# Turning W inside the sort and ordering layer 1 part by part in a two-layer conditional kernel

## The reference

```python
# x: 128 x 64 x 512; itok_B_0_7 ("subject") and itok_B_0_6 ("adapter"): one index in 0..7 and 0..6 per batch item
out0 = einsum('bct,bcd->bdt', x, w[subject]) + bias[subject][:, :, None]        # w: 8 x 64 x 64
x = x + out0
H = einsum('btd,od->bto', x, W)                                                # W: 512 x 512
xa = einsum('btd,brd->btr', x, A[adapter])                                     # A: 8 x 16 x 512
x = x + H + einsum('btr,bor->bto', xa, Bm[adapter]) * scalings[adapter]        # Bm: 8 x 512 x 16
```

## Time and profile before

| | us |
|---|---|
| median of 3 runs (246.84 to 247.28) | 247.12 |
| the profiled execution | 246.9 |
| its span, first to last instruction | 245.2 |
| TensorE busy in the span | 231.0 |
| VectorE, ScalarE, GpSimd busy | 148.5, 109.9, 71.7 |

### The profile page before, as it was taken

One profiled execution on the slowest core, in us unless ns is written; L12 is line 12 of the kernel. 1 busy time (PEld: TensorE's weight loads), 2 busy tenths in 40 slices (PEclk: granted clock), 3 DMA queues, 4 the chain that ended last, 5 costly groups with the idle time before them and its releaser, 6 DMA issues.

```text
span 245.2 us, 9843 instructions
## 1 busy us (share of the span) xinstructions
PE 231.0 (94%) x2917; PEld 188.8 (77%) x2919; DVE 148.5 (61%) x258; ACT 109.9 (45%) x191; POOL 71.7 (29%) x280
## 2 busy tenths in 40 slices
PE   1889999999999999999999999999999999999990
PEld 1667888888887888888888888888888888887750
DVE  6778856774457736775457736675457735345642
ACT  3265462552535353552535353562536343444621
POOL 3456501560046301560045501564134330000000
PEclk9999999999999999999999999999999999999998
DMA  6846564745465574745456563746455463641323
GB/s 143 264 137 144 172 179 130 208 118 166 135 178 141 153 192 110 215 121 178 125 164 152 150 196 107 210 114 192 127 153 161 136 195 111 199 124 45 88 54 77
DMA packets 23621, 36.56 MB, mean 149 GB/s; under 512 B 6066, under 2 KB 6066, under 8 KB 23602
## 3 DMA queue, kind: packets, MB, share of 16 engines
q1 hardware_dynamic: 16544, 26.36, 39.2%
q10 hardware_dynamic: 7058, 9.97, 14.1%
HBM read 19.53 MB, written 16.78 MB: 148 GB/s over the span
## 4 chain that ended last, share of the span: by engine, by line
PE 83%; DVE 6%; ACTq 2%; DMA 2%; issue 2%; ACT 2%; POOL 0%; SPq 0%; DVEq 0%; POOLq 0%
PE ps L851 66%; PE ps L820 13%; PE ps L796 3%; DMA x_ring<-in_x_dram 2%; ACTq L237 1%; DVE x_lo L529 1%; PE ps L755 1%; ACTq L675 1%; DVE o_ring L548 1%; DVE o_ring L544 1%; DVE m_lo L512 1%; ACT x_hi L640 1%; DVE x L521 1%; ACT m_f L662 0%; PE ps L790 0%
## 5 line engine op out<-in xcount | busy, mean ns | idle before, releaser
L851 PE MATMUL ps<-m_hi,x_hi 128*128 x248 | 99.4, 401 | 0.0
L851 PE MATMUL ps<-m_hi,x_lo 128*128 x248 | 96.8, 390 | 0.0
L851 PE MATMUL ps<-m_lo,x_hi 128*128 x248 | 96.6, 390 | 0.0
L529 DVE TENSOR_TENSOR x_lo<-x,x_hi 128x512 fp32r<-128x512 f32 x64 | 44.5, 696 | 62.7 <-ACT x_hi L640 62.6
L368 POOL COPY p_pair<-p_all 64x64 f32 x128 | 40.0, 313 | 124.5 <-DVE x L521 89.4
L640 ACT ACTIVATE x_hi<-x 128x512 fp32r<-128x512 f32 x64 | 40.4, 632 | 52.6 <-ACT o_ring L653 29.1
L653 ACT ACTIVATE o_ring<-ps 128x512 f32<-128x512 f32 x60 | 35.8, 596 | 56.7 <-PE ps L851 56.6
L851 PEld LDWEIGHTS ps<-m_hi,x_hi 128*128 128x128 f32 x248 | 46.6, 188 | 10.4 <-issue 0.2
L851 PEld LDWEIGHTS ps<-m_hi,x_lo 128*128 128x128 f32 x248 | 46.5, 188 | 10.1
L851 PEld LDWEIGHTS ps<-m_lo,x_hi 128*128 128x128 f32 x248 | 46.6, 188 | 9.1
L521 DVE TENSOR_TENSOR x<-ps,bias_pair 128x512 f32<-128x512 f32 x64 | 43.8, 686 | 9.1 <-PE ps L820 7.5
(11 more groups left out here) (101 smaller groups left out, 84.3 us busy)
## 6 DMA issues: line engine op xcount, KB each, us to landing
x_ring<-in_x_dram SPq DMA_DIRECT2D x124, 128.0 KB, 2.7
out_dram<-o_ring ACTq DMA_DIRECT2D x64, 128.0 KB, 2.6
out_dram<-o_ring SPq DMA_DIRECT2D x64, 128.0 KB, 2.3
a_f<-in_L_cond_A_dram SPq DMA_DIRECT2D x8, 128.0 KB
o_ring<-in_L_cond_W_dram SPq DMA_DIRECT2D x2, 256.0 KB, 4.3
o_ring<-in_L_cond_W_dram ACTq DMA_DIRECT2D x2, 256.0 KB, 5.6
x_ring<-in_x_dram ACTq DMA_DIRECT2D x4, 128.0 KB, 3.3
b_nat<-in_L_cond_Bm_dram ACTq DMA_DIRECT2D x1, 256.0 KB, 3.8
```

What stands on the lines that cost most here:

```text
L529: nc.vector.tensor_tensor(x1_lo[:, u % HELD], x1[:, u % 2], x1_hi[:, u % HELD], ALU.subtract).then_inc(x1_lo_ready, 1)
L851: mm = nc.tensor.matmul(ps[:, 2 + u % 2, :], part, m_tile(m, k, c), start=(c == 0 and part is hi and m is m_hi), stop=(c == TC - 1 and par ...
```

## The change

Five things are changed.

- **Loads.** SyncE issues W block 0, W block 1, w, and then the bias, which ScalarE issued before. ScalarE loads both halves of pair 0's x after reading two words instead of four; SyncE loads pair 1's after two words and pairs 2 and 3 after four more. Before, each engine loaded a half of pairs 0 and 1, and SyncE read eight words first.
- **W.** The four transposes of block 0 stand ahead of the sort's first table matmul (L761), those of block 1 ahead of the `place` matmul (L765); blocks 2 and 3 stay behind `turn_b(0)`.
- **M.** The low parts of tiles 2 and 3 of the first M are made by TensorE: it adds minus the high part to the sum in PSUM with a negated identity (`minus`, one new VectorE instruction), and ScalarE copies the rest out. VectorE keeps tiles 0 and 1.
- **Layer 1.** The order is now all four high x high, four high x low, four low x high; the wait for the low part of x1 stands ahead of the last four. Pair 0 has an order of its own, `layer1_first`. VectorE's list is changed too: `x1_add(1)` now follows `m_split_first(0)`, `m_split_first(1)` and `x1_split(0)`.
- **GpSimd** reads a pair's two table words while it places the pair before.

```diff
@@ sync, beginning @@
-            sp.dma_start(w_nat[:, 0, :], W[0:P, :]).then_inc(w_in[0], 16)
+            for o in range(2):
+                sp.dma_start(w_nat[:, o, :], W[o * P:o * P + P, :]).then_inc(w_in[o], 16)
             sp.dma_start(p_all[:], w.rearrange("s c d -> c s d")).then_inc(w0_in, 16)
-            sp.dma_start(w_nat[:, 1, :], W[P:2 * P, :]).then_inc(w_in[1], 16)
+            sp.dma_start(bias_all[:], bias...to_broadcast([P, S * C])...).then_inc(bias_in, 16)
@@ sync, x @@
-            b = words(sp, regs, batch[0:1, 0:2 * L0_QUAD], B - 1)
-            for i in range(2):
-                load_half(sp, i, 0, b[2 * i], x_first[i])
+            load_x(sp, 1, words(sp, regs[:2], batch[0:1, 2:4], B - 1), x_first[1])
+            b = words(sp, regs[:4], batch[0:1, 4:8], B - 1)
             for i in range(2, XR):
-                load_x(sp, i, b[2 * i:2 * i + 2], x_first[i])
+                load_x(sp, i, b[2 * i - 4:2 * i - 2], x_first[i])
@@ gpsimd, step @@
                 place_p(1)
+                if not isinstance(j, int) or j + 1 < PAIRS:
+                    ahead = 2 * ((u + 1) % 2)
+                    pool.load(regs[ahead:ahead + 2], table[0:1, ds(j * 4 + (4 + W_SUBJECT), 2)])
                 pool.wait_ge(pair_ready, j * 4 + 1)
@@ vector @@
             nc.vector.memset(a_parts[GR:P, :].bitcast(F32), 0.0).then_inc(zeroed, 1)
+            nc.vector.tensor_scalar(minus[:], ident[:], -1.0, None, ALU.mult).then_inc(zeroed, 1)
             dve.wait_ge(ids_in, 16)
...
             x1_add(0, 0)
             m_split_first(0)
+            m_split_first(1)
+            x1_split(0, 0)
             x1_add(1, 1)
-            x1_split(0, 0)
-            m_split_first(1)
-            m_split_first(2)
-            m_split_first(3)
+            x1_add(2, 2)
             x1_split(1, 1)
-            x1_add(2, 2)
             x1_add(3, 3)
             x1_split(2, 2)
             a_split(1)
+            b_split(1)
             x1_split(3, 3)
-            b_split(1)
@@ scalar @@
-            b = words(act, regs, batch[0:1, 0:4], B - 1)
-            for i in range(2):
-                load_half(act, i, 1, b[2 * i + 1], x_first[i])
+            load_x(act, 0, words(act, regs[:2], batch[0:1, 0:2], B - 1), x_first[0])
...
             x1_round(0, 0)
             m_round_first(1)
-            x1_round(1, 1)
             m_round_first(2)
             m_round_first(3)
+            for chunk in range(2, TC):
+                act.wait_ge(m_rest, chunk - 1)
+                nc.scalar.activation(m_lo[:, chunk * T:chunk * T + T], ps[:, FIRST + chunk, :],
+                                     ACT.Copy).then_inc(m_rest_ready, 1)
+            x1_round(1, 1)
             act.wait_ge(l0_done, XR)
@@ tensor @@
+            pe.wait_ge(w_in[0], 16)
+            for c in range(TC):
+                turn_w(0, c)
             pe.wait_ge(firsts_ready, 1)
...
+            pe.wait_ge(w_in[1], 16)
+            for c in range(TC):
+                turn_w(1, c)
             pe.wait_ge(place_ready, 1)
...
-            def layer1(j, u, k, tiles_awaited=False):
+            def layer1(j, u, k):
+                hi, lo = x1_hi[:, u % HELD], x1_lo[:, u % HELD]
                 for c in range(TC):
+                    nc.tensor.matmul(ps[:, 2 + u % 2, :], hi[:, c], m_tile(m_hi, k, c), start=c == 0, stop=False)
+                for c in range(TC):
+                    nc.tensor.matmul(ps[:, 2 + u % 2, :], hi[:, c], m_tile(m_lo, k, c), start=False, stop=False)
+                pe.wait_ge(x1_lo_ready, j + 1)
+                for c in range(TC):
+                    mm = nc.tensor.matmul(ps[:, 2 + u % 2, :], lo[:, c], m_tile(m_hi, k, c),
+                                          start=False, stop=c == TC - 1)
+                mm.then_inc(l1_done, 1)
+
+            def layer1_first(k):
+                pe.wait_ge(m_ready, 1)
+                for c in range(TC):
+                    pe.wait_ge(m_hi_ready, c + 1)
+                    nc.tensor.matmul(ps[:, 2, :], x1_hi[:, 0, c], m_tile(m_hi, k, c), start=c == 0, stop=False)
+                for c in range(2, TC):
+                    nc.tensor.matmul(ps[:, FIRST + c, :], minus[:], m_hi[:, c * T:c * T + T],
+                                     start=False, stop=True, skip_group_check=True).then_inc(m_rest, 1)
+                pe.wait_ge(m_ready, TC)
+                for c in range(2):
+                    nc.tensor.matmul(ps[:, 2, :], x1_hi[:, 0, c], m_tile(m_lo, k, c), start=False, stop=False)
+                pe.wait_ge(x1_lo_ready, 1)
+                for c in range(TC):
+                    nc.tensor.matmul(ps[:, 2, :], x1_lo[:, 0, c], m_tile(m_hi, k, c), start=False, stop=False)
+                for c in range(2, TC):
+                    pe.wait_ge(m_rest_ready, c - 1)
+                    mm = nc.tensor.matmul(ps[:, 2, :], x1_hi[:, 0, c], m_tile(m_lo, k, c),
+                                          start=False, stop=c == TC - 1)
```

More of the change, by code:

```diff
@@ L92, in cond_residual_layers @@
         ident_b = sb("ident_b", [P, P], BF16)
+        minus = sb("minus", [P, P], F32R)
         nothing = sb("nothing", [P, P], BF16)
@@ L336, in _ @@
             pool.wait_ge(bnat_in, 16)
-            regs = [pool.alloc_register(f"pool_word{i}") for i in range(2)]
+            regs = [pool.alloc_register(f"pool_word{i}") for i in range(4)]
+            order_reg = [pool.alloc_register("pool_place")]
             def dup_b(i):
-                k, = words(pool, regs[:1], order[0:1, ds(i, 1)], K - 1)
+                k, = words(pool, order_reg, order[0:1, ds(i, 1)], K - 1)
                 if isinstance(i, int) and i == 0:
@@ L356, in _ @@
             pool.wait_ge(others_ready, 2)
+            pool.load(regs[0:2], table[0:1, W_SUBJECT:W_SUBJECT + 2])
             def step(j, u, n):
@@ L361, in step @@
                 at_least(pool, x1_ready, j - (PR - 1 if n is None else min(PR - 1, HEAD - 1 + (u - HEAD) % BODY)))
-                s = words(pool, regs, table[0:1, ds(j * 4 + W_SUBJECT, 2)], S - 1)
+                s = [pool.snap(r, min_val=0, max_val=S - 1) for r in regs[2 * (u % 2):2 * (u % 2) + 2]]
                 if n is None and j == 0:
@@ L552, in _ @@
             dve.wait_ge(consts, 11)
-            dve.wait_ge(zeroed, 2)
+            dve.wait_ge(zeroed, 3)
             dve.wait_ge(w0_in, 16)
@@ L605, in _ @@
                 act.dma_start(w_nat[:, o, :], W[o * P:o * P + P, :]).then_inc(w_in[o], 16)
-            act.dma_start(bias_all[:], bias.rearrange("s d -> (s d)").rearrange("(a n) -> a n", a=1)
-                          .to_broadcast([P, S * C]).rearrange("p (s d) -> p s d", s=S)).then_inc(bias_in, 16)
             regs = [act.alloc_register(f"act_word{i}") for i in range(4)]
@@ L772, in _ @@
             turn_b(0)
-            pe.wait_ge(w_in[0], 16)
             for c in range(TC):
-                turn_w(0, c)
-            for c in range(TC):
-                for o in (2, 3, 1):
+                for o in range(2, TC):
                     if c == 0:
@@ L841, in m_tile @@
                 return m[:, ds(k * (TC * T) + c * T, T)]
-            def layer1(j, u, k, tiles_awaited=False):
+            def layer1(j, u, k):
+                hi, lo = x1_hi[:, u % HELD], x1_lo[:, u % HELD]
                 for c in range(TC):
-                    if tiles_awaited:
-                        pe.wait_ge(m_ready, c + 1)
-                    hi = x1_hi[:, u % HELD, c, :]
-                    lo = x1_lo[:, u % HELD, c, :]
-                    for part, m in ((hi, m_hi), (hi, m_lo), (lo, m_hi)):
-                        mm = nc.tensor.matmul(ps[:, 2 + u % 2, :], part, m_tile(m, k, c),
-                                              start=(c == 0 and part is hi and m is m_hi),
-                                              stop=(c == TC - 1 and part is lo))
+                    nc.tensor.matmul(ps[:, 2 + u % 2, :], hi[:, c], m_tile(m_hi, k, c), start=c == 0, stop=False)
[6 more added lines that the diff above has]
+                mm.then_inc(l1_done, 1)
@@ L911, in step @@
                         layer1(j, u, k[0])
+                elif n is None and j == 0:
+                    layer1_first(k[0])
                 else:
-                    layer1(j, u, k[0], tiles_awaited=n is None and j == 0)
+                    layer1(j, u, k[0])
                 if n is None and j == 0:
```

10 lines of the change are left out of this document (7 added, 3 removed).

## The result

The changed kernel takes 250.94 us (median of 4 runs, 250.49 to 252.41), the kernel before 247.09 beside it: ratio 1.016, 95% interval 1.0136 to 1.0184. That is 3.85 us slower. The forecast was 248.8, slower by 1.7, with a range up to 250.4: the direction is right, the size is not. The profiled execution took 250.49 us with a span of 248.7; before it was 246.9 and 245.2.

What follows compares the result with a forecast made beforehand. TensorE, full from 24 to 225 us, bounds the kernel, so its entry into that stretch counts: 0.9 (layer 1 late) + 0.45 (two matmuls) - 0.3 (wait filled) + 0.65 (b_parts wait) = 1.7, giving 248.8, range 247.2 to 250.4.

Steps and rivals of the forecast that it cites:

- x of pair 0: Beginning: x issued by ScalarE at 8.0 and 8.65, landed at 12.05; layer 0 starts at 12.1 instead of 12.74.
- A: Load of a_f, issued 0.15 later behind the bias on SyncE: lands at 10.9; bounds nothing and 1.2 later.
- First M: ScalarE's m_hi(0) starts 1.16 after layer 0, at 13.25: 0.65 gained.
- a rival at 0.06: TensorE's clock falls to 1.2 GHz over longer pauses, layer 1 of pair 0 up to 3.2 slower: 250.4, chance 0.06.
- VectorE's new order: x1_add(1) waits behind m_lo(1) and x_lo(0), starting at 16.13; layer 1 at 17.6, 0.9 later than before.
- Two matmuls more: The added `minus` matmuls on TensorE cost 0.45.
- ScalarE's new order: Later b_parts (23.3, before 21.27) decides the second M's products: 24.8, 1.7 later than 23.12.
- the other two terms: Ahead of the second M's products: former wait filled, -0.3, and a new wait for b_parts, +0.65.
- At nothing: GpSimd's early words, the earlier bias issue and the split waits in steady layer 1 cost and gain nothing.

Runs made afterwards that it cites:

- b_xsplit: Kernel before, ScalarE loading both halves of pair 0's x and SyncE both of pair 1's, words read as before: 249.54 us, 1.0088.
- a_turns_back: Changed kernel with all 16 transposes of W behind turn_b(0) again: 250.43 us, 1.0131.
- b_xloads: Kernel before with only the x loads of the changed kernel: 250.1 us, 1.0104.
- a_warm: Changed kernel plus five matmuls on a zero tile ahead of layer 0 of pair 0: 252.19 us, 1.0195.
- b_add1_late: Kernel before with x1_add(1) put behind m_split_first(1) and x1_split(0), nothing else: 249.57 us, 1.0083.
- a_front_back: Changed kernel with its whole beginning (loads, W turning, x loads) as before: 249.43 us, 1.007.
- a_all_early: Changed kernel with its whole beginning as before and x1_add(1) right behind m_split_first(0): 247.36 us, 0.9996.
- b_parts: As a run: kernel before with only the steady layer 1 (all pairs but pair 0) part by part: 247.39 us, 1.0009.
- b_w_behind: Kernel before with only W block 1 issued ahead of w on SyncE: 247.77 us, 1.0018.
- a_combo: Changed kernel with x1_add(1) early, x loads as before, and five zero matmuls ahead of layer 0 of pair 0: 249.09 us, 1.0063.
- experiment 2: Changed kernel with x1_add(1) moved back right behind m_split_first(0): 250.61 us, 1.0146.
- b_xswap: Kernel before, ScalarE loading pair 0's x, half 1 ahead of half 0, SyncE pair 1's, words as before: 248.06 us, 1.0032.
- a_xloads_back: Changed kernel with only the x loads as before: 249.78 us, 1.0063.
- b_front: Kernel before with the loads, turned W blocks and x loads of the changed kernel: 250.02 us, 1.0085.

## Why the prediction was wrong in size

**What failed.** The step "x of pair 0" (landed at 12.05, layer 0 at 12.1) measured 13.22 and 13.26: 1.16 of the missing 1.6. It was made of two numbers. The second half was issued at 9.26 instead of 8.65: the place matmul came at 7.00 instead of 6.76, behind W block 1's transposes, ScalarE's load of two words took 0.71 where 0.66 had to cover the load and more, and its two issues took 1.42 and not 1.24. And that half took 4.0 to land instead of 3.4. The 3.4 was chosen between two prices of the earlier trace rows, and the lower one, 3.0, was no landing: before, both halves of pair 0 counted on one semaphore from two queues, its 32 updates came mixed from 10.13 to 12.69, and the view puts the sixteenth (11.01) down to ScalarE's half. What the row shows for sure is that the pair was there at 12.69, 4.2 behind the later issue. For the same reason 3.0 and 4.2 do not bear out what step "A" reads from them ("the two landing times of the x halves agree"). No row stood for a second half behind the first on one queue. The runs with the x loads alone bear out the direction (+2.9 us, of which layer 0 shows 1.4), and b_xsplit puts the time on the exchange.

**The clock.** "First M" took m_hi(0) as 1.16 behind layer 0 and measured 1.89: 0.73 more. The pause of 1.98 ahead of layer 0 was forecast, the 1.2 GHz after it was a rival at 0.06. That the pause brought the clock down is not shown, for the engine was not at the full pace before it. A row of the weight loads, near the end of the turning:

```profile
10.44 0.34 PEld L751 LDWEIGHTS ps<-ident,o_ring 128*128 128x128 f32 x2
```

That is 0.17 each, where before the last three took 0.10 each. What stood in neither the sum nor the rivals is this: before, the full pace came only with the last transposes, and it can be missing. a_turns_back had layer 0 at half pace behind a pause of 1.03, b_xloads at the full pace behind 1.96. The rival had its price at layer 1 of pair 0; it fell on the first M's products. a_warm removes just this part (1.16 again) and shows the other place where the rival would have struck.

**What held.** "VectorE's new order": m_hi(0) to layer 1 was forecast as 4.35 and measured 4.40, with m_lo(1), x_lo(0) and x1_add(1) one behind another as forecast. b_add1_late and the pair a_front_back and a_all_early price it alone at 2.3 and 2.1. That the sum fits so well in the changed kernel is partly luck: on the slow engine layer 0 of pair 1 ended at 17.29 and x1_add(1), which needs it, started at 18.10, so there the order can have cost 0.8 at most (an estimate from these two times), and the slow engine would have cost the rest of the 1.59 anyway. (The text of the forecast says 0.9 later: that is 1.54 less the 0.64 it had gained ahead.) "Two matmuls more": 0.45, measured 20.59 to 21.04. "A" (a_f rounded at 10.9): 11.01; the bound of 1.2 later did not come in the changed kernel.

**Smaller.** "ScalarE's new order" let b_parts decide when the second M starts. b_parts started 5.16 behind layer 1 (19.55 to 24.71) where 5.7 was forecast, and TensorE waited only 0.16 for it. Forecast 0.79, measured 0.45, which is what the two matmuls cost. Neither of the other two terms came: the wait ahead of the products was neither filled nor longer (0.18 before, 0.16 after). The holes in the instruction stream (about 0.4 in after) were in no term.

**At nothing.** It holds for the split waits (b_parts) and for the sum of the remaining parts (a_all_early). It does not hold for w behind W block 1, to which the forecast gave no term at all: neither w nor Bm, which lands later with it, was followed. In after the loss lies hidden under the later x; alone it is 0.55 (b_w_behind), through Bm and the turning. Through w and GpSimd's words it shows in a_combo, as 0.3.

**How the losses add.** The beginning alone costs 2.6, the order alone 2.0 (a_front_back), together 4.6; measured are 3.85. The overlap, as far as the traces show it, is that a late, slow start moves x1_add(1)'s own input back (experiment 2).

**Open.** Why TensorE reaches the full pace before layer 0 in some executions and not in others. Why the halves land later when one queue carries a pair: the runs exclude the earlier issue and, as the whole cause, the shared partitions. Nor is it shown why TensorE's unchanged instructions pause in the full stretch of b_xloads, b_xsplit and b_xswap. That the holes follow transfers of the instruction queue was seen, not tested.

## What to carry to other kernels

When a load is moved to another queue, ask for the landing of the same place in the queue, not of the same queue: the second transfer behind a sibling is another row. Where two transfers count on one semaphore, trust only the time of the last. When an instruction is moved down in a list, look for a second engine that still waits for its first position. When a pause of TensorE appears in a forecast, ask at what pace it worked before the pause. And when two losses may lie over one another, undo each in the changed kernel and do each alone in the old one: here undoing the order in after won 0.3, and doing it alone in before cost 2.3.

## What the runs showed of the hardware

- Behind some pauses of TensorE of about 2 us its clock fell. The windows of a_front_back, whose pause of 1.99 ended at 18.43:

```profile
17.00:19.00 2.00, 0.57 (x32) 1.00 0.45 133
19.00:20.00 1.00, 1.00 (x13) 0.68 0.50 174
20.00:21.00 1.00, 1.00 (x4) 0.50 0.71 227
...
23.00:24.00 1.00, 1.00 (x6) 1.00 0.22 53
```

The granted clock goes to 0.50 (1.2 GHz) only behind the pause, when the matmuls run again, and comes back by 23. Behind the pauses of 2.08 in a_xloads_back and 2.06 in a_warm it fell too, behind b_add1_late's of 1.92 and b_xloads' of 1.96 it stayed at 1.00. These are single executions; the two groups of b_add1_late's times suggest that the same code falls in one execution and not in another, so no limit can be read from them. The Trainium skill ("TensorE: Matmul & The Clock Gate", Why this matters for your kernels) warns of idle gaps between bursts of matmuls; these traces agree with the warning.
- The column of the granted clock can read 1.00 where the engine runs at half pace. Between 14.32 and 16.3 us of the changed kernel it reads 1.00 while products are 0.43 apart; in a_front_back this pace had 0.50 beside it (20.00 to 21.00 above). The spacing of equal matmuls is the surer sign.
- A register load of two words out of `batch` took 0.70 to 0.71 us on ScalarE (after, a_turns_back, b_front, b_xloads) where one of four took 0.52 (before, a_xloads_back, a_all_early, b_xsplit). Fewer words were slower.
